# Graph network on one Trainium2 core: the second mixing product taken with its weights loaded and its messages streamed

## The reference

```
alpha = concat(K_v[dst] * K_v[src], K_v[dst] * K_E) * scale     # 128 values
gate  = sigmoid(layernorm(alpha) * ln_g[h] + ln_b[h])
m     = (concat(V_v[src], V_E) @ Wu[h] + bu[h]) * gate          # 128 values
m     = leaky(layernorm(m @ Wm[h] + bm[h]) * mln_g[h] + mln_b[h])   # 64 values
head  = segment_sum(m, dst)
```

## Time and profile before

| | |
|---|---|
| median of 3 runs | 17780.12 us (17768.55 to 17810.48) |
| the profiled execution | 17803.45 us |
| its span in the trace | 17801.3 us |
| layer 1 (`sweep1`), first to last iteration | from 2962 to 11448 us of the span |

### The profile page before, as it was taken

How to read it: one execution, slowest core, us unless ns; L and a number is a source line. 1 busy time by engine, 2 the same in 40 slices (tenths; PEclk the granted TensorE clock), 3 DMA queues, 4 the chain that set the end, 5 groups by cost and what they waited for, 6 DMA issues and landing times.

```text
span 17801.3 us, 231614 instructions
## 1 busy us (share of the span) xinstructions
PE 11205.7 (63%) x52461; PEld 8279.5 (47%) x52462; DVE 10797.0 (61%) x29437; ACT 5021.6 (28%) x10532; POOL 10715.0 (60%) x10914
## 2 busy tenths in 40 slices
PE   5333335888888888888888888733333355555565
PEld 4222223666666565656566656522222233333454
DVE  7222225888888888888888888732222333333776
ACT  0000002555555555555555555400000011111000
POOL 0666664666666666666666666556666566666000
PEclk9999998888888888888888888755555555555555
DMA  0000002222222222222222222100000111111111
GB/s 25 22 22 22 22 22 70 62 63 64 61 62 63 64 62 62 62 62 62 62 62 62 62 63 64 42 22 22 22 22 22 29 46 46 46 46 46 51 48 40
DMA packets 474914, 838.02 MB, mean 47 GB/s; under 512 B 151155, under 2 KB 264980, under 8 KB 472725
## 3 DMA queue, kind: packets, MB, share of 16 engines
q0 software_dynamic: 310272, 637.61, 13.3%
q1 hardware_dynamic: 164116, 195.98, 3.6%
HBM read 755.78 MB, written 77.21 MB: 47 GB/s over the span
## 4 chain that ended last, share of the span: by engine, by line
DVE 30%; issue 27%; POOL 24%; PE 13%; DVEq 4%; POOLq 1%; ACT 1%; DMA 0%; SPq 0%; ACTq 0%
POOL arena L1096 22%; DVE acc L406 5%; DVE arena L529 4%; PE psum L977 4%; DVE arena L618 2%; DVE arena L588 2%; PE psum L939 2%; DVE arena L523 2%; PE psum L954 2%; DVE arena L561 2%; PE psum L947 2%; DVEq L329 1%; POOL idx_src L1103 1%; DVE arena L607 1%; DVE arena L603 1%
## 5 line engine op out<-in xcount | busy, mean ns | idle before, releaser
L1096 POOL DMA_INDIRECT arena<-table,idx_src x6464 | 6216.8, 962 | 4461.7 <-DVE arena L523 1803.1
L406 DVE TENSOR_TENSOR acc<-acc,psum 64x128 f32 (+2 forms) x6464 | 2041.1, 316 | 4230.0 <-PE psum L904 3019.2
L904 PE MATMUL psum<-arena 128*64 128x128 f32 x6464 | 1585.9, 427 | 3274.3 <-DMA arena<-table,idx_src 3274.3
L904 PEld LDWEIGHTS psum<-arena 128*64 128x64 f32 x6464 | 1266.1, 223 | 3593.9 <-issue 3569.1
L781 ACT ACTIVATE arena<-arena 128x128 f32<-128x128 f32 x6464 | 2648.8, 483 | 620.2 <-DVE arena L609 620.2
L1096 POOL DMA_INDIRECT arena<-table1q,idx_dst x1616 | 1873.1, 1159 | 492.3 <-issue 492.3
L787 ACT ACTIVATE arena<-psum,cols 128x512 f32<-128x512 f32 x1616 | 1256.1, 777 | 3047.8 <-PE psum L947 3044.6
L964 PEld LDWEIGHTS psum<-wm,arena 128*128 128x128 f32 x12928 | 1742.0, 202 | 560.2 <-issue 464.4
L954 PE MATMUL psum<-arena,wvu 128*128 128x512 f32 x3232 | 1966.9, 695 | 1.4 <-DVE arena L535 1.4
L964 PE MATMUL psum<-wm,arena 128*128 128x64 f32 x12928 | 1797.5, 285 | 0.1
L761 ACT ACTIVATE small<-small 128x49 f32<-128x49 f32 (+1 forms) x7 | 1.6, 233 | 6252.5 <-DVE small L365 3716.9
(11 more groups left out here) (171 smaller groups left out, 14815.5 us busy)
## 6 DMA issues: line engine op xcount, KB each, us to landing
arena<-table,idx_src POOLq DMA_INDIRECT x6464, 2.4
kept_rows<-arena SPq DMA_DIRECT2D x404, 132.0 KB, 1.7
arena<-kept_rows SPq DMA_DIRECT2D x404, 132.0 KB, 2.1
arena<-in_edge_t SPq DMA_DIRECT2D x404, 128.0 KB, 2.8
arena<-table1q,idx_dst POOLq DMA_INDIRECT x1616
table<-arena SPq DMA_DIRECT2D x7, 1120.0 KB, 4.2
table1q<-arena SPq DMA_DIRECT2D x7, 896.0 KB, 6.4
table<-arena SPq DMA_DIRECT2D x2, 1568.0 KB, 5.1
```

What stands on the lines that cost most here:

```text
L406: V.tensor_tensor(at_, at_, sums, ALU.add).then_inc(added, 1)
L904: last = M.matmul(psum[0:D, z, t * WIN:(t + 1) * WIN], rows[s][:, t, :], onehot[z][:, t, :], start=True, stop=True)
L1096: K.indirect_dma_start(out=dst[:, t, :], out_offset=None, in_=table, in_offset=bass.IndirectOffsetOnAxis(ap=idx[:, t:t + 1], axis=0)).then ...
```

## The change

`o_pair` is replaced by `mix` and `turn_o`. In `mix(j)` the loaded operand is `Wm[h]` (128x64) and the streamed one the gated messages of a whole group (512 columns), for heads 2j and 2j+1, whose results go to partitions 0 to 63 and 64 to 127 of bank 6. ScalarE's new `shift_o(j)` moves that to SBUF and adds the bias, which now is one value per partition. `turn_o(j)` transposes the result back, tile by tile, into bank 0, which it shares with `turn_x`; `take_o(j)` reads it there. The order of the parts in the queues changes with it, and `o_sb`, `y` and `msg` hold their parts in the order (pair of heads, tile, head of the pair).

```diff
 # TensorE
 turn_x:  after(pe, xt_ready, i)
+         after(pe, o_taken, 2 * (i - 2))
-def o_pair(j): ... (16 products of 64 streamed columns, 4 bias products, in two calls)
+def mix(j):
+    pe.wait_ge(gm_ready, H * (i - 1))
+    after(pe, o_fm_ready, 2 * (i - 2) + j)
+    for half in range(2):
+        h = 2 * j + half
+        last = M.matmul(psum[half * D:(half + 1) * D, 6, :], wm[:, h, :],
+                        gm[z][:, h, :, :].rearrange("p t n -> p (t n)"), start=True, stop=True)
+    last.then_inc(mixed, 1)
+def turn_o(j):
+    pe.wait_ge(o_fm_ready, 2 * (i - 2) + j + 1)
+    if now[0]:
+        pe.wait_ge(xt_ready, i + 1)
+    after(pe, o_taken, 2 * (i - 2) + j)
+    for t in range(G):
+        last = M.transpose(psum[:, 0, t * P:(t + 1) * P], o_fm[j][:, t, :], ident[:, :])
+    last.then_inc(o_done, 1)
 # TensorE's order in an iteration
 turn_x, edge_k(0),
+mix(0),
 turn(0), m_u(0), edge_k(1), turn(1), m_u(1),
-o_pair(0),
+turn_o(0), mix(1),
 turn(2), m_u(2), sums(0),
+turn_o(1),
 turn(3), m_u(3),
-o_pair(1),
 sums(1)
 # ScalarE
+def shift_o(j):
+    act.wait_ge(mixed, 2 * (i - 2) + j + 1)
+    A.activation(o_fm[j].rearrange("p t n -> p (t n)"), psum[:, 6, :], ACT.Identity,
+                 bias=bm_cols[:, j:j + 1]).then_inc(o_fm_ready, 1)
 take_o(j): ps = psum[:, 6 -> 0, :]
 # ScalarE's order in an iteration
 norm 1, sigmoid(0), norm 2, copy of xt,
+shift_o(0),
 sigmoid(1), norm 3,
-sigmoid(2), take_o(0), sigmoid(3),
+take_o(0), shift_o(1), sigmoid(2), sigmoid(3),
 norm 0 of the next group, take_o(1)
 # GpSimd: affine with weight and bias broadcast in the new order of the parts
+y4 = y[z].rearrange("p (j t h) d -> p j t (h d)", j=2, t=G)
+weight, bias = (v[:, :].rearrange("p (j n) -> p j n", j=2).unsqueeze(2).to_broadcast([P, 2, G, P])
+                for v in (mg, mb))
 # once, ahead of the sweeps
-ones3, bm_up, bm_part, bm_parts: the bias cut into three bf16 parts, 3 DMAs of a row each
+bm_cols [P, 2]: 2 DMAs that lay the centred bias along the partitions
```

More of the change, by code:

```diff
@@ L126, in gnn @@
         bm_rest = sb("bm_rest", [1, H, D])
[L127 to L130, removed]
+        bm_cols = sb("bm_cols", [P, 2])
         mg = sb("mg", [P, H * D])
@@ L199, in gnn @@
         gm = [view(H * G * P, [H, G, P]) for _ in range(2)]
+        o_fm = [view(G * P, [G, P]) for _ in range(2)]
         o_sb = [view(G * H * D, [G * H, D]) for _ in range(2)]
@@ L286, in gnn @@
         gm_ready = sem("gm_ready")
+        mixed = sem("mixed")
+        o_fm_ready = sem("o_fm_ready")
         o_done = sem("o_done")
@@ L447, in _ @@
             link(V.tensor_tensor(bm_rest[:, :, :], bm_row[:, :, :],
[L448 to L454, removed]
+                                 small[0:1, 0:H].unsqueeze(2).to_broadcast([1, H, D]), ALU.subtract), mark="bm_parts")
             dve.wait_ge(dinv_in, 16 * 3)
@@ L770, in _ @@
             dve_done("sweep1")
+            act.wait_ge(bm_in, 32)
             def sweep1(i, k, s, inside):
@@ L788, in sigmoid @@
                                  bias=cols[:, 2, h:h + 1], scale=cols[:, 1, h:h + 1]).then_inc(gated, 1)
+                def shift_o(j):
+                    act.wait_ge(mixed, 2 * (i - 2) + j + 1)
+                    A.activation(o_fm[j].rearrange("p t n -> p (t n)"), psum[:, 6, :], ACT.Identity,
+                                 bias=bm_cols[:, j:j + 1]).then_inc(o_fm_ready, 1)
                 def take_o(j):
                     act.wait_ge(o_done, 2 * (i - 2) + j + 1)
[L792 to L795, removed]
+                    part = slice(2 * j * G, 2 * (j + 1) * G)
+                    ps = psum[:, 0, :].rearrange("p (q d) -> p q d", d=D)
+                    A.activation(o_sq[z][:, part, :], ps, ACT.Square)
+                    A.activation(o_sb[z][:, part, :], ps, ACT.Copy).then_inc(o_taken, 1)
                 if now[1]:
@@ L805, in sweep1 @@
                                  ACT.Copy).then_inc(xt_ready, 1)
+                if now[2]:
+                    shift_o(0)
                 if now[1]:
@@ L812, in sweep1 @@
                     take_o(0)
+                    shift_o(1)
                 if now[1]:
+                    sigmoid(2)
                     sigmoid(3)
@@ L976, in sums @@
                             at_ = (t % 2 * 2 + half) * WIN
+                            part = (half * G + t) * 2
                             last = M.matmul(psum[:, 7, at_:at_ + WIN],
-                                            msg[z][:, t * H + 2 * half:t * H + 2 * half + 2, :].rearrange("p h d -> p (h d)"),
+                                            msg[z][:, part:part + 2, :].rearrange("p h d -> p (h d)"),
                                             onehot[z][:, t, :], start=True, stop=True)
@@ L984, in sweep1 @@
                     edge_k(0)
+                if now[2]:
+                    mix(0)
                 if now[1]:
@@ L993, in sweep1 @@
                 if now[2]:
-                    o_pair(0)
+                    turn_o(0)
+                    mix(1)
                 if now[1]:
@@ L999, in sweep1 @@
                     sums(0)
+                if now[2]:
+                    turn_o(1)
                 if now[1]:
@@ L1002, in sweep1 @@
                     m_u(3)
-                if now[2]:
-                    o_pair(1)
                 if now[4]:
@@ L1175, in _ @@
             dve_done("bm_parts")
-            for i in range(3):
-                sp.dma_start(bm_parts[i:i + 1, :], bm_part[i][:, :]).then_inc(bm_in, 16)
+            for p in range(2):
+                sp.dma_start(bm_cols[:, p:p + 1], bm_rest[0:1, 2 * p:2 * p + 2, :].rearrange("o h d -> o (h d)")
+                             ).then_inc(bm_in, 16)
             dve_done("t0")
```

26 lines of the change are left out of this document (6 added, 20 removed).

## The result

| | before | after |
|---|---|---|
| median of 5 runs | 17782.75 us | 17881.88 us (17877.25 to 17891.81) |
| span of the profiled execution | 17801.3 us | 17887.6 us |

The ratio is 1.0054, 95% interval 1.0039 to 1.0069: the kernel became 0.54% slower, some 99 us, where +1.6% (18060 us) was forecast. Sign and range held; the likeliest case and its size didn't. Spread over 404 iterations 99 us is 0.25 us each, against 0.70 forecast.

A forecast was written before the change was run, and what follows sets the result against it. It took VectorE's own order plus the round trip through `sums(1)` as the bound. 0.70 us over 404 iterations, +283, less 2, gave 18084 on the profiled 17803, so 18060 us as median; range 17790 to 18300.

The forecast's parts named there:

- Sign: Whole kernel: slower at 0.82, same at 0.07, faster at 0.11.
- the step that counts: `mix(0)` ahead of `turn(0)`: new TensorE work where it has little room before `gate_m(0)`, 0.70 us per iteration, +283 us.
- I take one after the other without a further gap, 1.7 and 3.4: `mix(0)`'s two heads stream in sequence, 1.7 us at high clock, 3.4 at low; likeliest case, 18060 us, chance 0.45.
- the halves overlap: Rival on `mix(0)`: three of four passes count, 1.28 us high; 0.44 us per iteration, +176 us, 17955 us, chance 0.25.
- the rooms: Slack ahead of `gate_m(0)`: 3.1 us high all along, 1.45 turned high, 2.3 after a jump, none low all along.
- The shares of the kinds of iteration: Of eight iterations, one is high all along, three turn high, two come after a jump, two are low.
- Turned high and behind a jump: `mix(0)` ahead of `gate_m(0)`: +0.45 us in three of eight iterations that turn high, +0.4 in two after the jump.
- Low without a jump: Low all along, no room ahead of `gate_m(0)`: +1.7 us, taken between 0.45 and 3.4, in two of eight iterations.
- The removal of `o_pair` worth nothing: Both `o_pair` stand behind `m_u(1)` and `m_u(3)`, where TensorE has time: 0; TensorE's total falls by 0.5 to 1.2 us.
- The rival on the other side: Clock stays high at `sums(1)`, `add(2)` waits 0.63 us less, -255 us: 17525 us; chance 0.10 for below 17745.
- GpSimd 0: GpSimd's same 1024 elements in four dimensions instead of three, with 1 us of room behind `affine`: 0.
- ScalarE 0: Two `shift_o` of 0.59 us on ScalarE; `sigmoid(1)` has 0.3 to 0.7 us of room: 0, up to +47 us.

The follow-up runs named there:

- mix_mid: Changed kernel with `mix(0)` behind `m_u(1)`, `mix(1)` behind `m_u(2)`, ScalarE's order moved along: 17700.59 us, 0.9968 of the kernel before; on two other chips 1.0299 and 1.0325.
- mix_behind: Changed kernel with `mix(0)` directly behind `m_u(0)` instead of ahead of `turn(0)`: 17846.61 us, 1.0053 of the kernel before.
- same_half: Changed kernel with both heads of a `mix` on the lower half, heads 0 and 2 lost: 17903.58 us, 1.0084 of the kernel before.
- fill3: Changed kernel with three more dense products ahead of `sums(1)`, results unused: 17855.19 us, 1.0057 of the kernel before.
- before_fill2: Kernel before with two dense products, results unused, ahead of `o_pair(1)`'s own: 17834.88 us, ratio 1.0045.
- mix0_twice: Changed kernel with `mix(0)`'s two products issued twice, same result: 19019.06 us, 1.0427 of the kernel before on the third chip.

## Why the prediction was wrong in size

**Where the time is paid: right.** `mix(0)` in the stretch ahead of `gate_m(0)` was called the step that counts. `mix_mid` takes it out of there, and the wait falls from 0.51 to 0.10 us and the slowdown with it; `mix_behind`, which moves nothing else, moves the wait one step on; with the old `o_pair(0)` in the same place `gate_m(0)` waits 2.3 us per iteration. The first two ran on chips without ScalarE's idle time and settle it for these; on two of the three others `mix_mid` was run and lost 3%, for another reason than `gate_m(0)`. The third ran only on the chips with that idle time, so its 1.9 us per iteration can't be split cleanly between the place and the chip.

**"I take one after the other without a further gap, 1.7 and 3.4": wrong, the step that failed.** The row next to it, `m_u`, has its two passes on the same columns, and its pattern was carried over to two products on different ones. Measured from start to next start: 1.01 and 1.90 us, and 1.86 and 3.61 when both are made to share one half (6031.12 to 6032.98, 6022.27 to 6025.88). The rival "the halves overlap" was the right mechanism, with 17955 us, though it too took `mix(0)` as longer than it is, three of four passes or 1.28 us high. With 1.01 and 1.90 us `mix(0)` fits the rooms of the iterations that turn high and of those behind a jump, and the two terms for them came to nothing.

**The shares of the kinds of iteration, taken as given: wrong too, which `same_half` shows.** That run is the forecast's own case, 1.86 and 3.61 us, and cost 150 us, not 283: `mix(0)` was low in only 38 of 280 iterations, against 112 in the changed kernel. So the share follows from the change, and the right length by itself would not have made the forecast's sum right.

**The sum by its terms.** Turned high and behind a jump, (3 x 0.45 + 2 x 0.4)/8 = 0.27 us were forecast, and nothing was paid. Low without a jump, 3.4/8 = 0.43 were forecast, and 94 of 280 paid 1.5 us, 0.51. The 0.10 us that `gate_m` waited before already were not taken off. So this wait grew by 0.41 us where 0.70 was forecast. The overlap rival's 0.44 looks like a hit beside 0.41, but by luck: it had 0.11 where nothing was paid and 0.33 where 0.51 was. The rest, from 0.41 to 0.25, are terms that the sum didn't have, and they come next.

**The removal of `o_pair` worth nothing: right.** TensorE's wait ahead of `sums(1)` grew from 2.3 to 1406.2/280 = 5.0 us per iteration; the saved work went there (817/404 = 2.0 us, where 0.5 to 1.2 was forecast). **A colder `sums(1)`: it came.** The prediction had the longer wait and no price for it. The clock is low behind it in every iteration now, and `add(2)` waits 0.15 us more, 60 us over the stage.

**Two terms that it lacked.** L543 0.23 us shorter, as it begins later within GpSimd's pass, and 0.09 us less ahead of the statistics. Without them the sum would have been 0.56 us, +1.3%. That the result lies as low as 0.25 us is thus not `mix(0)`'s price alone: 0.56 us were lost, and 0.32 given back by terms that the prediction didn't have.

**The rival on the other side: it didn't come, and its price is open.** It was said that the wait grows, so the clock can't stay high, and at `sums(1)` that is what happened. The mean clock rose all the same, to 0.86. `fill3` and `before_fill2` have the mean at 0.89 and 0.86, and nothing was gained: in `fill3` an earlier `add(2)` mostly started L543 further into GpSimd's multiplication, in `before_fill2` `add(2)` wasn't earlier. That the rival's 0.63 us are not to be had even at 1.0 isn't shown.

**GpSimd 0: right as to its end,** but not as to its effect on VectorE, which the term didn't ask for. **ScalarE 0: right on the chips of the result** (`sigmoid(0)` is late in 23 of 280 iterations, and only behind `mix(0)`), wrong on the three others.

## What to carry to other kernels

Work that is taken off an engine is worth what the wait behind it is worth, and work that is added costs where it stands: ask first for the stretch in which the other engine catches up, and put the new product behind it. Two fp32 products that use separate halves of the array's columns took hardly longer than one here and should be costed as one, and the granted clock's share should be taken as a result of the change, not as a given: here a `mix` made twice as long went with a higher clock on one chip (`same_half`), and a doubled `mix(0)` with none on another (`mix0_twice`). Before pulling an operation of VectorE forward, look at what GpSimd reads at that moment. Try an order that gains a few tenths of a per cent on more than one chip before keeping it.

## What the runs showed of the hardware

**Column halves in fp32 run fully side by side.** Four records 1.08 us at 2.4 GHz and 1.97 at 1.2, against 1.93 and 3.67 on one half. The Trainium skill, TensorEngine Tiling (Array Packing), Key Properties, says that different tiles work in parallel; these rows agree. It says as well that a change of mode drains the array: the next product starts 1.01 us behind the start of `mix(0)` and the estimate for its two streamed passes was 0.85, so some 0.16 us at the high clock would be the drain by that estimate; behind an `m_u` without such a change the next product starts after 0.86 us in the kernel before (6026.34 to 6027.20). That it is the drain that takes this time was not tested by itself.

**VectorE's and GpSimd's three-operand passes over SBUF exclude each other.** VectorE's takes 3.36 us for 1.23 when GpSimd starts first, and GpSimd's 3.34 for 2.35 when VectorE does. The Trainium skill, SBUF — State Buffer, SBUF: two separate sides, calls this an exclusive lock and not a shared bandwidth, held by whoever starts first; the two rows agree.

**The kernel before takes about 17750 us on some chips and 18230 to 18280 on others,** and on those each of the ten traces (none of them of the kernel before) has ScalarE standing still ahead of one activation in most iterations, 3.3 to 6.2 us on the mean, with no releaser on the core. The cause is open.
